# The softmax loop of a two-layer graph network with sixteen slots for gathered rows and indices made eleven groups ahead

## The chip, the cores and the metric

The kernel runs on one core of a Trainium2 chip. The metric is the device time of one execution, in microseconds; lower is better. Three runs are given for the kernel before.

## The reference

There are 6250 nodes with 128 features and 100,000 edges, sorted by destination. Two layers follow each other, each added to its input and normalised:

```python
def L0(h, e, fc_w, attn, rel, src, dst):
    f = (e @ fc_w.T).reshape(-1, 4, 128)
    feat = jnp.sum(jax.nn.leaky_relu(attn[rel] * f, negative_slope=0.2), axis=1)
    return jax.ops.segment_sum(h[src] + feat, dst, num_segments=h.shape[0])

def L1(features, edge_index, W, b, a1_w, a1_b, a2_w, a2_b):
    h = features @ W.T + b
    s1, s2 = h @ a1_w + a1_b[0], h @ a2_w + a2_b[0]
    src, dst = edge_index
    e = s1[src] + s2[dst]
    e = jnp.where(e >= 0, e, 0.01 * e)
    m = jax.ops.segment_max(e, src, num_segments=n)
    ex = jnp.exp(e - m[src])
    att = ex / jax.ops.segment_sum(ex, src, num_segments=n)[src]
    return jax.ops.segment_sum(att[:, None] * h[dst], src, num_segments=n)

x = layernorm(x + L0(x, edge_attr, fc_w, attn, edge_type, src, dst))
x = layernorm(x + L1(x, (src, dst), W, b, a1_w, a1_b, a2_w, a2_b))
```

## The kernel before

Five engines run a program each and meet at semaphores. In the profile PE is TensorE, DVE is VectorE, ACT is ScalarE, POOL is GpSimd and SP issues plain transfers. The kernel has three parts: the edge loop (the first layer, and the sorting of the edges by source), a middle that normalises and computes the rows `h` with the two scores of each node, and the softmax loop (the second layer), followed by the last normalisation.

The softmax loop goes over groups of 512 edges (`TG` = 4 tiles of 128) that belong to one block of 122 source nodes. All groups take the same path:

- ScalarE copies the four index columns of a group into `idx1` (`idx`, L668), `AHEAD` = 5 groups before the group's own step, and counts that in `i1_ready`. It also copies the block's score (`block_s1`, L674).
- GpSimd (`group1`, L546) waits for `i1_ready` and for `o_done` of the group eight before, whose slot it takes, and issues four indirect transfers. Each gathers 128 rows of `h_rows`, 130 floats wide, into slot `k` of `hg`, and adds to `g_in[k]` as it lands.
- TensorE (`rows`, L885) waits for the landing and spreads the destination scores over a 128 by 512 tile, two groups ahead of the group's own step. VectorE takes the maximum over it (`maximum`, L1306), with a penalty that ScalarE made (L682) from a membership matrix (`members`, L1263).
- VectorE updates the running maximum. TensorE (`back`, L896) sends it back to the edges. Two steps later VectorE forms the exponents (`edge_parts`, L1279, and on), ScalarE takes the exponential and scales the gathered rows in their slot (`scale`, L701).
- Three steps later TensorE sums the scaled rows by source (`attend`, L906) and counts `o_done`. Five steps later VectorE adds that into the block's result (`update`, L1273). `o_done` frees the slot for GpSimd at the same time.

Each engine works through its own steps in a fixed order. In step g TensorE does `rows(g + 2)`, `back(g)`, `attend(g - 3)`; VectorE does `update(g - 5)`, then the maximum of g and the exponents of g - 2, then `members(g + 2)`; ScalarE does `idx(g + 5)`, `penalty(g + 2)`, then `probs` and `scale` of g - 2, then `decays(g - 1)`. The sums and maxima of two successive groups use two PSUM areas in turn (`rows_of`, `back_of`, `sums_of`).

`hg` has `S1` = 8 slots in the tile `room`. The tile `arena` holds `h_sb`, the rows as they were computed, until they are written to `h_rows`; the result of the loop stands behind them. The number of groups is known only at run time: it is the number of live groups, rounded up to a multiple of `S1`, and the code is written out for `G1_LEAST` groups but for one stretch in a loop, whose count is read from `more_groups`.

## Time and profile before

| | us |
|---|---|
| median of three runs | 3019.51 |
| lowest and highest | 3010.88, 3020.82 |
| the profiled execution's own time | 2996.43 |
| its span, first to last instruction | 2994.6 |
| softmax loop, first gather to last update | 1666.67 to 2943.45 |

The profile is of one execution. The chain of work that ended last is cut short in this page, at the last few instructions, so it says nothing here; the timeline has to be read in its place. A start in the timeline is when an engine began an instruction; the idle time in brackets is how long it had nothing to do before, with what ended that by the semaphore records. "remote" and "issue" name no instruction. The ends of TensorE's records are modelled. Waits that GpSimd spends are not named: its idle time is put down to "issue".

### The profile page before, as it was taken

The numbers are of one execution on the slowest core, as the hardware profiler recorded it, in microseconds if no ns is written. First come the engines' busy times: TensorE is split into PE (matmuls) and PEld (weight loads), VectorE is DVE, ScalarE is ACT, GpSimd is POOL, SyncE is SP. The second block draws the span as 40 slices with busy tenths as digits, with TensorE's granted clock in tenths as the row PEclk, the third lists the DMA queues.
The fourth block names the chain that finished last, engine by engine and source line by source line (L and its number), as shares of the span: only waits on it lengthen the run. The fifth ranks groups of instructions, "written<-read, shape, count | busy, mean of one in ns | idle before, by whom it ended". The sixth has DMA issues, their size and how long they took to land. (4 is left out here: it accounts for less than half of the span.)

```text
span 2994.6 us, 44539 instructions
## 1 busy us (share of the span) xinstructions
PE 2386.8 (80%) x11705; PEld 1541.4 (51%) x11705; DVE 2350.5 (78%) x5910; ACT 1525.4 (51%) x4524; POOL 2000.6 (67%) x1839
## 2 busy tenths in 40 slices
PE   5899999999999999999997366666666666666662
PEld 2355555555555555555555355555555555555551
DVE  8899999999999999999999455555554555555557
ACT  0366666666666666666665334343343433443433
POOL 0388788778887888888785566666666666666660
PEclk9999999999999999999999665566655666666665
DMA  2233333333333333333332323332232222333322
GB/s 87 67 98 99 95 97 98 99 99 96 97 97 99 98 97 96 96 99 99 99 95 63 79 67 69 65 69 66 65 68 66 68 66 66 69 67 67 66 61 47
DMA packets 156606, 244.12 MB, mean 82 GB/s; under 512 B 40837, under 2 KB 84399, under 8 KB 156227
## 3 DMA queue, kind: packets, MB, share of 16 engines
q0 software_dynamic: 58624, 108.72, 16.7%
q1 hardware_dynamic: 97730, 132.55, 15.3%
q8 instruction: 97, 1.59, 0.2%
q14 instruction: 155, 1.26, 0.1%
HBM read 231.99 MB, written 9.12 MB: 81 GB/s over the span
## 5 line engine op out<-in xcount | busy, mean ns | idle before, releaser
L503 POOL DMA_INDIRECT room<-in_x,pks x784 | 1013.5, 1293 | 351.8 <-issue 238.3
L546 POOL DMA_INDIRECT room<-h_rows,idx x832 | 785.0, 943 | 476.6 <-issue 457.6
L798 PE MATMUL FP<-fc_sb,room 128*128 128x512 f32 x1568 | 834.5, 613 | 4.5 <-DMA room<-in_e 4.5
L597 ACT ACTIVATE w_sb<-WP 128x512 f32<-128x512 f32 x784 | 468.1, 597 | 502.6 <-PE WP L807 306.0
L885 PE MATMUL FP<-ident,room 128*128 128x128 f32 x1664 | 385.8, 405 | 359.2 <-DMA room<-h_rows,idx 224.8
L807 PE MATMUL WP<-at_p,rel_oh 100*128 100x512 bf16 x2352 | 637.7, 379 | 1.7 <-issue 1.7
L885 PEld LDWEIGHTS FP<-ident,room 128*128 128x128 f32 x1664 | 332.4, 297 | 410.6 <-DMA room<-h_rows,idx 255.2
L682 ACT ACTIVATE accT<-accT,neg_big 128x512 f32<-128x512 bf16 x208 | 150.0, 721 | 762.6 <-DVE accT L1263 417.1
L807 PEld LDWEIGHTS WP<-at_p,rel_oh 100*128 100x128 bf16 x2352 | 228.3, 97 | 546.9 <-issue 452.4
L1111 DVE TENSOR_TENSOR z<-FP,w_sb 128x1024 f32<-128x1024 f32 x392 | 479.9, 1224 | 20.8 <-issue 12.3
L1118 DVE SCALAR_TENSOR_TENSOR y<-z 128x2048 f32<-128x2048 f32 x196 | 447.9, 2285 | 0.0
L798 PEld LDWEIGHTS FP<-fc_sb,room 128*128 128x128 f32 x1568 | 267.6, 190 | 70.5 <-DMA room<-in_e 4.7
L701 ACT ACTIVATE room<-room,pr 128x129 f32<-128x129 f32 x832 | 266.6, 392 | 6.8
L1126 DVE TENSOR_TENSOR hs<-y 128x1024 f32<-128x1024 f32 x196 | 238.4, 1216 | 0.0
L604 ACT ACTIVATE boh<-arena,rank_pay 128x52 f32<-128x52 bf16 x784 | 237.2, 375 | 0.0
L514 POOL DMA_INDIRECT sorted_edges<-runs,ridx x196 | 184.1, 939 | 64.9 <-issue 60.8
L817 PEld LDWEIGHTS AP<-doh,room 128*128 128x128 f32 x1568 | 206.3, 192 | 35.2 <-DVE room L1142 6.8
L1273 DVE SCALAR_TENSOR_TENSOR arena<-arena,decay,FP 128x129 f32 x104 | 36.0, 346 | 214.6 <-remote 131.1
L817 PE MATMUL AP<-doh,room 128*128 128x64 f32 x1568 | 197.4, 269 | 6.6 <-DVE accT L1102 4.4
L1273 DVE SCALAR_TENSOR_TENSOR arena<-arena,decay,AP 128x129 f32 x104 | 35.9, 346 | 204.0 <-remote 142.8
L1306 DVE CUSTOM_DVE_ANT_0 hs<-accT,FP 128x512 f32<-128x512 f32 x208 | 141.8, 682 | 29.4 <-issue 21.8
L1263 DVE TENSOR_TENSOR accT<-z,WP 128x512 bf16<-128x512 bf16 x208 | 141.5, 681 | 0.7 <-DVE room L1256 0.7
(222 smaller groups left out, 3071.2 us busy)
## 6 DMA issues: line engine op xcount, KB each, us to landing
room<-in_e SPq DMA_DIRECT2D x196, 256.0 KB
rel_sb<-in_rel_g SPq DMA_DIRECT2D x196, 200.0 KB
z<-sorted_sources SPq DMA_DIRECT2D x208, 128.0 KB
room<-h_rows,idx POOLq DMA_INDIRECT x832
room<-in_x,pks POOLq DMA_INDIRECT x784
sorted_edges<-runs,ridx POOLq DMA_INDIRECT x196
accT<-in_x_t SPq DMA_DIRECT2D x1, 3125.0 KB, 9.8
h_rows<-arena SPq DMA_DIRECT2D x13, 227.5 KB, 2.8
```

The costliest lines, as they stand in the source:

```text
L503: pool.indirect_dma_start(xg[:, k, u, 0:P], None, x[:, :], bass.IndirectOffsetOnAxis(ap=pks[:, k, u:u + 1], axis=0)).then_inc(xg_in[k], 16)
L546: pool.indirect_dma_start(hg[k][:, u, :], None, h_dram[:, :], bass.IndirectOffsetOnAxis(ap=idx1[:, k, u:u + 1], axis=0)).then_inc(g_in[k], 16)
L597: nc.scalar.activation(w_sb[:, u // 2, u % 2, :], WP[u % 2][:, :], ACT.Copy).then_inc(w_copied, 1)
L604: ins = nc.scalar.activation(boh[:, k % 2, u, :], onehot[:, :, bass.ds(g * TG + u, 1)].rearrange("p b o -> p (b o)"), ACT.Identity, bias=0 ...
L701: nc.scalar.activation(hg[k][:, u, 0:P + 1], hg[k][:, u, 0:P + 1], ACT.Identity, bias=0.0, scale=pr[:, k % 2, u:u + 1]).then_inc(h_scaled, 1)
L798: mm = pe.matmul(FP[u // 2][:, u % 2, :], e_sb[:, k, u, :], fc_sb[:, :], start=True, stop=True)
L807: mm = pe.matmul(WP[u % 2][:, :], rel_oh[:, k % 2, u * P:(u + 1) * P], at_p[:, j, :], start=(j == 0), stop=(j == 2))
L817: mm = pe.matmul(AP_[:, 0:W], msg[:, k % 2, u, :], doh[:, k % 2, u, :], start=(u == 0), stop=(u == TG - 1))
L885: mm = pe.matmul(rows_of(k)[:, u * P:(u + 1) * P], hg[k][:, u, P + 1:P + 2].to_broadcast([P, P]), ident[:, :], start=True, stop=True)
L1111: v.tensor_tensor(z[:, h, :, :], FP[h][:, :, :], w_sb[:, h, :, :], ALU.mult).then_inc(z_done, 1)
L1118: v.scalar_tensor_tensor(y[:, :, :, :], z[:, :, :, :], SLOPE0, z[:, :, :, :], ALU.mult, ALU.max).then_inc(y_done, 1)
L1126: v.tensor_tensor(hs[:, :, :], y_all[:, :, 0:D4 // 2], y_all[:, :, D4 // 2:D4], ALU.add).then_inc(hs_done, 1)
```

## The change

`S1` becomes 16 and `AHEAD` 11. Eight of the slots stay in `room`; the other eight lie in `arena`, over `h_sb`, which is dead once its rows are written and its last column is transposed (`n_s1t`, for which GpSimd now waits before its first gather). Each slot has its own semaphore and its own column set of `idx1` and `mparts`. The written-out stretches and the loops are rearranged for multiples of sixteen; the waits that count through a slot's semaphore use `G_IN` (4 a group) in place of 8. VectorE's loop had four steps a pass and registers for the slot; now it has sixteen steps and fixed slots. `LAG`, the number of PSUM areas and the order of each engine's step stay.

```diff
-G1 = 8 * -(-(G0 + NS) // 8)
-G1_LEAST = 8 * -(-G0 // 8)
+S1 = 16
+G1 = S1 * -(-(G0 + NS) // S1)
+G1_LEAST = S1 * -(-G0 // S1)
...
-S1 = 8
 LAG = 5
-AHEAD = 5
-D1 = 4
+AHEAD = 11
+IN_ROOM = 8
+G_IN = 16 * TG // S1
...
-        hg_all = room[:, 0:S1 * TG * HROW].rearrange("p (s u k) -> p s u k", s=S1, u=TG)
-        hg = [hg_all[:, k, :, :] for k in range(S1)]
+        hg = [f[:, j * TG * HROW:(j + 1) * TG * HROW].rearrange("p (u k) -> p u k", u=TG)
+              for f, n in ((room, IN_ROOM), (arena, S1 - IN_ROOM)) for j in range(n)]
...
             more = group_count(pool)
+            pool.wait_ge(n_s1t, 1)
             for k in range(S1):
                 group1(k, k, True)
-            for g in range(S1, G1_LEAST):
+            for g in range(S1, G1_LEAST - S1):
                 group1(g, g % S1, False)
-            with pool.Fori(G1_LEAST, pool.snap(more + (G1_LEAST - S1 + 1)), S1) as i:
+            with pool.Fori(G1_LEAST - S1, pool.snap(more + (G1_LEAST - S1 + 1)), S1) as i:
...
-                    act.wait_ge(g_in[k], 16 * TG + (g - k - S1) * 8)
+                    act.wait_ge(g_in[k], 16 * TG + (g - k - S1) * G_IN)
...
-                pe.wait_ge(g_in[k], 16 * TG + (g - k) * 8)
+                pe.wait_ge(g_in[k], 16 * TG + (g - k) * G_IN)
...
-            with dve.Fori(G1_LEAST - S1, dve.snap(more + (G1_LEAST - 2 * S1 + D1 + 1)), D1) as i:
-                half = dve.snap(i & (S1 - D1))
-                other = dve.snap(S1 - 2 - half)
-                for k in range(D1):
-                    step1(i + k, k, False, half + k, half + (k - 2) if k >= 2 else other + k)
+            with dve.Fori(G1_LEAST - 2 * S1, dve.snap(more + (G1_LEAST - 2 * S1 + 1)), S1) as i:
+                for k in range(S1):
+                    step1(i + k, k, False, k, (k - 2) % S1)
```

The loops of SP, ScalarE and TensorE are changed in the same way as GpSimd's.

## Rows read from the trace of the kernel before

**Rows 1.** Windows: PE, PEld, DVE, ACT, POOL busy (instructions), PEclk, DMA, GB/s.

```profile
200.00:1500.00 1300.00, 1300.00 (x6138) 674.32 (x6137) 1292.82 (x1534) 858.74 (x2215) 1039.66 (x852) 1.00 0.36 97
1800.00:2800.00 1000.00, 635.78 (x3316) 568.75 (x3315) 542.05 (x2813) 393.59 (x1489) 626.83 (x665) 0.61 0.30 67
```

**Rows 2.** Grouped lines, 1800 to 2800 us; last, all gathers on the page.

```profile
L546 POOL DMA_INDIRECT room<-h_rows,idx x665 | 627.2, 943 | 372.3 <-issue 372.3
L885 PE MATMUL FP<-ident,room 128*128 128x128 f32 x1328 | 307.5, 404 | 267.3 <-DMA room<-h_rows,idx 162.0 <-DVE vmax L1306 79.5 <-issue 25.3
...
L1273 DVE SCALAR_TENSOR_TENSOR arena<-arena,decay,FP 128x129 f32 x83 | 28.7, 346 | 183.0 <-remote 119.7 <-PE AP L906 52.7 <-issue 10.6
...
L1273 DVE SCALAR_TENSOR_TENSOR arena<-arena,decay,AP 128x129 f32 x82 | 28.3, 346 | 166.4 <-remote 120.6 <-PE FP L906 41.5 <-issue 4.2
...
L546 POOL DMA_INDIRECT room<-h_rows,idx x832 | 785.0, 943 | 476.6 <-issue 457.6
```

**Rows 3.** Timeline, 2110 to 2152 us: start, duration, idle before in brackets.

```profile
2110.95 2.07 PE L885 MATMUL FP<-ident,room 128*128 128x128 f32 x8 [4.18 <-DMA room<-h_rows,idx]
...
2112.97 2.07 PE L906 MATMUL FP<-room,hs 128*128 128x129 f32 x8
...
2117.44 0.94 POOL L546 DMA_INDIRECT room<-h_rows,idx  x1 [0.30 <-issue]
...
2120.78 0.35 DVE L1273 SCALAR_TENSOR_TENSOR arena<-arena,decay,FP 128x129 f32 x1 [8.05 <-remote]
...
2121.40 0.94 POOL L546 DMA_INDIRECT room<-h_rows,idx  x1 [3.02 <-issue]
...
2128.32 2.08 PE L885 MATMUL FP<-ident,room 128*128 128x128 f32 x8 [2.31 <-DMA room<-h_rows,idx]
...
2130.34 2.07 PE L906 MATMUL AP<-room,w_sb 128*128 128x129 f32 x8
...
2138.78 0.35 DVE L1273 SCALAR_TENSOR_TENSOR arena<-arena,decay,AP 128x129 f32 x1 [1.83 <-remote]
...
2139.40 0.94 POOL L546 DMA_INDIRECT room<-h_rows,idx  x1 [3.32 <-issue]
...
2151.53 0.94 POOL L546 DMA_INDIRECT room<-h_rows,idx  x1 [2.45 <-issue]
```

**Rows 4.** Timeline of the loop's start: GpSimd, VectorE and TensorE.

```profile
1666.67 1.04 POOL L546 DMA_INDIRECT room<-h_rows,idx  x1 [5.22 <-issue]
...
1685.04 0.29 PE L896 MATMUL EP<-mparts,accT 128*128 128x6 bf16 x4
...
1694.22 0.69 DVE L1306 CUSTOM_DVE_ANT_0 hs<-accT,FP 128x512 f32<-128x512 f32 x1 [11.35 <-issue]
...
1704.57 0.18 DVE L1279 TENSOR_REDUCE sm<-EP 128x8 f32<-128x24 f32 x1 [9.65 <-remote]
...
1705.53 0.94 POOL L546 DMA_INDIRECT room<-h_rows,idx  x1 [0.30 <-issue]
...
1711.83 0.69 DVE L1306 CUSTOM_DVE_ANT_0 hs<-accT,FP 128x512 f32<-128x512 f32 x1 [4.84 <-issue]
...
1714.76 0.68 DVE L1306 CUSTOM_DVE_ANT_0 hs<-accT,FP 128x512 f32<-128x512 f32 x1
...
1717.52 0.94 POOL L546 DMA_INDIRECT room<-h_rows,idx  x1 [11.04 <-PE AP L906]
...
1717.94 0.68 DVE L1306 CUSTOM_DVE_ANT_0 hs<-accT,FP 128x512 f32<-128x512 f32 x1
```

**Rows 5.** Timeline of GpSimd's group 16, its last gather, and the last update.

```profile
1764.89 0.94 POOL L546 DMA_INDIRECT room<-h_rows,idx  x1 [0.30 <-issue]
...
2922.07 0.94 POOL L546 DMA_INDIRECT room<-h_rows,idx  x1 [0.30 <-issue]
...
2943.10 0.35 DVE L1273 SCALAR_TENSOR_TENSOR arena<-arena,decay,FP 128x129 f32 x1 [1.28 <-PE FP L906]
```

**Rows 6.** Timeline of ScalarE: an index copy.

```profile
2140.54 0.19 ACT L668 ACTIVATE idx<-y 128x4 int32<-128x4 int32 x1
```

More of the change, by code:

```diff
@@ L194, in build @@
         mT = accT[:, 0:SLOTS * GE // 2].bitcast(BF16).rearrange("p (s k) -> p s k", s=SLOTS)
-        pen = accT[:, S1 * GE // 2:S1 * GE // 2 + SLOTS * GE].rearrange("p (s k) -> p s k", s=SLOTS)
-        hg_all = room[:, 0:S1 * TG * HROW].rearrange("p (s u k) -> p s u k", s=S1, u=TG)
-        hg = [hg_all[:, k, :, :] for k in range(S1)]
+        pen = accT[:, SLOTS * GE:2 * SLOTS * GE].rearrange("p (s k) -> p s k", s=SLOTS)
+        hg = [f[:, j * TG * HROW:(j + 1) * TG * HROW].rearrange("p (u k) -> p u k", u=TG)
+              for f, n in ((room, IN_ROOM), (arena, S1 - IN_ROOM)) for j in range(n)]
         z_flat = z[:, 0, :, :].rearrange("p a k -> p (a k)")
@@ L218, in build @@
         ge = msg_flat[0:NS, 2 * G1:3 * G1]
-        s1_parts = msg_flat[:, TG * HROW:TG * HROW + 2 * G1].bitcast(BF16)[:, 0:G1 * PARTS3].rearrange(
+        s1_parts = msg_flat[:, TG * HROW:TG * HROW + 3 * G1 // 2].bitcast(BF16)[:, 0:G1 * PARTS3].rearrange(
             "p (g c) -> p g c", c=PARTS3)
@@ L472, in _ @@
             more = group_count(sp)
-            for g in range(RSLOTS, G1_LEAST):
+            for g in range(RSLOTS, G1_LEAST - S1):
                 sources(g, g % S1, False)
-            with sp.Fori(G1_LEAST, sp.snap(more + (G1_LEAST - S1 + 1)), S1) as i:
+            with sp.Fori(G1_LEAST - S1, sp.snap(more + (G1_LEAST - S1 + 1)), S1) as i:
                 for k in range(S1):
@@ L725, in _ @@
                 step1(k, k, True)
-            for g in range(S1, G1_LEAST - S1):
+            for g in range(S1, G1_LEAST - 2 * S1):
                 idx(g + AHEAD, (g + AHEAD) % S1, False)
@@ L729, in _ @@
                 step1(g, g % S1, False)
-            with act.Fori(G1_LEAST - S1, act.snap(more + (G1_LEAST - 2 * S1 + 1)), S1) as i:
+            with act.Fori(G1_LEAST - 2 * S1, act.snap(more + (G1_LEAST - 2 * S1 + 1)), S1) as i:
                 for k in range(S1):
@@ L922, in _ @@
                 step1(k, k, True)
-            for g in range(S1, G1_LEAST - S1):
+            for g in range(S1, G1_LEAST - 2 * S1):
                 step1(g, g % S1, False)
-            with pe.Fori(G1_LEAST - S1, pe.snap(more + (G1_LEAST - 2 * S1 + 1)), S1) as i:
+            with pe.Fori(G1_LEAST - 2 * S1, pe.snap(more + (G1_LEAST - 2 * S1 + 1)), S1) as i:
                 for k in range(S1):
@@ L1285, in edge_sum @@
                 v.tensor_tensor(el[:, 0, :], sm[:, :, 0],
-                                hg_all[:, bass.ds(at, 1), :, P + 1].rearrange("p o u -> p (o u)"),
+                                hg[at][:, :, P + 1],
                                 ALU.add).then_inc(edge_summed, 1)
@@ L1382, in _ @@
                 step1(k, k, True, k, k - 2)
-            for g in range(S1, G1_LEAST - S1):
+            for g in range(S1, G1_LEAST - 2 * S1):
                 step1(g, g % S1, False, g % S1, (g - 2) % S1)
-            with dve.Fori(G1_LEAST - S1, dve.snap(more + (G1_LEAST - 2 * S1 + D1 + 1)), D1) as i:
-                half = dve.snap(i & (S1 - D1))
-                other = dve.snap(S1 - 2 - half)
-                for k in range(D1):
-                    step1(i + k, k, False, half + k, half + (k - 2) if k >= 2 else other + k)
+            with dve.Fori(G1_LEAST - 2 * S1, dve.snap(more + (G1_LEAST - 2 * S1 + 1)), S1) as i:
+                for k in range(S1):
+                    step1(i + k, k, False, k, (k - 2) % S1)
             for k in range(S1):
```

## The prediction

> **What bounds the kernel now.** I read the windows of the two large loops first, then the grouped lines of the softmax loop with the waits ahead of them, and at last its timeline. The edge loop is full of arithmetic: VectorE works 1292.82 of 1300 us and TensorE all of it. In the softmax loop no engine is full: in 1000 us VectorE works 542 us, TensorE 636, GpSimd 627, and the granted clock is 0.61, that is, mostly the lower of its two levels, 1.2 GHz [rows 1]. In those 1000 us 665 gathers are issued, four to a group, so a group takes 6.0 us. A gather is 943 ns on GpSimd and stands 0.30 us behind the one before it when nothing holds it, 1.25 us in all, 5.0 us a group. The idle time ahead of the gathers is 372.3 us; 665 x 0.30 = 200 of it is that spacing and 172 are pauses, 1.0 us a group [rows 2].
>
> The same rows name two suspects. TensorE waits 162.0 us for gathered rows to land before L885 (0.97 us a group), and VectorE is idle 183.0 + 166.4 = 349 us before the update L1273, which needs the sum of TensorE (o_done) [rows 2]. The timeline tells what kind of wait the second is. By its count L1273 at 2120.78 is group 67's; TensorE's sum for that group, L906, began at 2112.97 and ends by its record at 2115.04. VectorE goes on 5.7 us after that, and GpSimd starts group 75 at 2121.40, 0.6 us after VectorE: both had waited for the same count. GpSimd's last gather had ended at 2118.38. The same is seen at 2138.78 and 2139.40, for the L906 that ended at 2132.41 [rows 3]. So a slot is not late because TensorE works on it; TensorE's completion becomes visible late, some 2.3 us after GpSimd has stopped issuing gathers. I call this the late signal. What causes it inside the chip no row tells. The rows of GpSimd in 1780 to 2300 us, counted in the timeline, come as bursts of 4, 8 or 12 gathers; a burst of 12 with its pause takes 18.0 us (2121.40 to 2139.40), one of 8 takes 12.1 us (2139.40 to 2151.53): 1.50 and 1.52 us a gather. A longer burst has a longer pause behind it [rows 3].
>
> The start of the loop is the run that matters most here. There eight slots are empty and GpSimd issues 32 gathers without a pause, 1666.67 to 1706.47. In these 40 us VectorE takes the maxima of three groups only, by its count: it stands 11.35 us before the third, at 1694.22, and 9.65 us before L1279 at 1704.57, whose sums TensorE had ended by its record at 1685.33. Once GpSimd is silent the maxima follow each other in 1714.76 to 1717.94, 3.2 us. GpSimd itself then waits 11.04 us for the first slot [rows 4]. Rows gathered far ahead did not make the arithmetic faster; the arithmetic stood still while they were gathered.
>
> **The change, part by part.** (1) *Slots, steady state.* GpSimd may run 16 groups ahead of the sums in place of 8. Since it is paced at 5.0 us and the loop at 6.0, it runs to its limit wherever that lies, and then it waits for the newest sum, as now. What goes is TensorE's wait for landings: two of the six L885 groups from 2110 to 2140 show it, with 4.18 and 2.31 us [rows 3]. The gain has bounds: at most 0.97 us a group (all of the 162 us), at least nothing. VectorE's waits in the same stretch, 8.05 and 1.83 us, end with the late signals [rows 3], and the pace was 1.5 us a gather for each length of burst. So I take the lower bound, no gain. Where the stall goes: TensorE's early maxima row is late no more, and the next thing late is again the sum's signal.
>
> (2) *The first burst.* It grows from 32 gathers to 64: 39.80 us becomes 64 x 1.25 = 80 us, so it ends at 1746.6. Indices do not stop it: eleven exist at once, and the next five need about the steps that VectorE managed in the burst before. Then GpSimd waits for the first sum. A pause of 11.04 us stood behind 32 gathers, 3.32 behind 12 [rows 3, 4]; for 64 I take 11 again (3 if the arithmetic got far enough in 80 us, 20 if the delay doubles with the burst). Group 16 then starts at 1757.6; now it starts at 1764.89 [rows 5]. GpSimd gains 7.3 us.
>
> (3) *The end.* After GpSimd's last gather, which ends at 2923.01 now, the arithmetic behind it takes until 2943.45, that is 20.4 us [rows 5]. With eight more groups standing gathered it has eight more steps to do, at 3.18 us of the undisturbed pace in [rows 4]: 25.4 us more. Bounds: 3.18 a step and, if TensorE at the low clock is the pace (L885 2.07, L896 0.29, L906 2.07 [rows 3, 4]), 4.4, which is 35 us.
>
> (4) *Small edits.* ScalarE makes six more index copies and constant copies before the loop; at 0.19 us each [rows 6] they stand in its wait for VectorE before 1666, and if that cover is gone they cost 2 us once. The wait of GpSimd for the transposition falls before its wait for the table's last writes: nothing. The number of groups is 208 in both (832 gathers divided by four is a multiple of sixteen [rows 2]), so no padding group is added. VectorE's loop over slots, one pass of sixteen in place of passes of four, has the same instructions: nothing, or a few tenths.
>
> Sum: 192 groups at the present pace 0, the start -7.3, the end +25.4, so +18 us. The profiled execution took 2996.43 us around a span of 2994.6; with the change it would be 3014.5. The runs shown lie 23 us above it, median 3019.51, so I forecast 3019.5 + 18 = 3037.5 us, 0.6% slower. A difference under 0.3%, 9 us, is about what a measurement of this kernel can't tell from no change (the three runs lie 10 us apart).
>
> The Trainium skill speaks for the change: "DMA: Bandwidth & Descriptors", section "Rules for kernel authors", says to issue a DMA early, do the work, and wait for it late, so that its fixed cost is overlapped. The landings in [rows 2] agree with it; the first burst in [rows 4] doesn't show the work being done meanwhile. By that rule alone the case would be rival A below.
>
> **Rivals.** A, *the landing wait was the pace*. Of groups three apart each waits for its gather, and each such gather waited for the sum that stood behind the maxima before it: a ring of slot, gather, landing, maxima, sum, 18 us long, that eleven groups of distance would open. For it: groups 72 and 75 (L885 at 2110.95 and 2128.32) waited for landings, three groups apart, and the pace is 18.0 us for three groups whatever the bursts [rows 3]. Against it: the late signal is most of that ring. If all of the 0.97 us goes, the pace is 5.0 us, which is GpSimd's too: 192 x 0.97 = 186 us less, +18, so 2851 us. If a third goes, 62 less, so 2975 us. It decides from 0.1 us a group upward.
>
> B, *fewer pauses*. In a burst of 32 with only as long a pause as a signal needs (5.4 us to L1306 at 1711.83), a group would take 45.4/8 = 5.7 us, so 192 x 0.3 = 58 us less: 2980 us. Against it: during that burst the arithmetic did three groups, not eight [rows 4].
>
> C, *the index becomes the wait*, on the slow side of my forecast. Indices were made three steps before a slot came free; with eleven against sixteen that is one step. ScalarE makes the index copy behind the penalty and scaling of the step before: the copy at 2140.54 comes 1.8 us after the update at 2138.78 whose sum frees the slot at the same distance [rows 3, 6]. Of the two restarts of GpSimd in the cycle the one at 2139.40 would start 1.8 us later; the copy for the one at 2121.40 was made before it. That is 1.8 us in five groups, 0.36 a group, 69 us: 3107 us. It decides where the copy ends after the signal and GpSimd has nothing queued. Against it: the pause lets the arithmetic go on, so half may come back (3070 us).
>
> D, *the burst starves the arithmetic for longer*: the pause behind 64 gathers is 20 us and the pace of the first 50.85 us (6.36 a group) returns now and then. One fifth of the time at it is 192 x 0.33 x 0.2 = 13, and 9 more in the pause: 3060 us.
>
> E, *the change doesn't take hold*: index counts keep GpSimd at its old distance. Then neither start nor end moves and the time is 3019. The eleven ready indices speak against it.
>
> **How the numbers follow.** Forecast (no steady gain, longer end) 0.42, its own range 3015 to 3055; A in full 0.08, A in part or B 0.25; C 0.12; D 0.08; E 0.05. Inside the forecast a tenth of a microsecond of gain per group eats the 18 us, so of its 0.42 I give 0.04 to faster, 0.13 to the same and 0.25 to slower. Faster: 0.04 + 0.33 = 0.37. Same: 0.13 + 0.05 + 0.01 of D = 0.19. Slower: 0.25 + 0.12 + 0.07 = 0.44. For 8 times in 10 the range goes from 2930 (A at half) to 3085 (C between its two values).
>
> **What would show it.** Right: an unbroken row of about 64 gathers at the start with fewer than eight maxima in it; then bursts with pauses as before, 133 gathers in 200 us; TensorE's wait for landings gone; L1273 still waiting for about 350 us in 1000; 40 to 50 us from the last gather to the last L1273. Wrong: over 140 gathers in 200 us and shorter waits at L1273 (A, B); GpSimd starting right behind L668 (C). If the late signal goes away when GpSimd no longer waits for it, my whole argument from the first burst falls.

## The result and the profile after

The changed kernel takes 3086.43 us (median of four runs, 3075.85 to 3092.7), the kernel before beside it 3017.56 (four runs, 3010.88 to 3020.82). The ratio is 1.023, with a 95% interval of 1.0208 to 1.0252: the change makes the kernel slower by 69 us. The forecast was 3037 us with a range to 3085, so the sign was right, the size was not, and the time lies a little over the range. The profile of the changed kernel is that of the execution of 3092.0 us.

The first view is that of the windows, with the columns of [rows 1].

```profile
200.00:1500.00 1300.00, 1298.45 (x6123) 671.74 (x6121) 1285.23 (x1531) 854.10 (x2208) 1039.73 (x850) 1.00 0.35 97
1800.00:2800.00 1000.00, 509.85 (x3171) 469.27 (x3172) 522.16 (x2689) 377.51 (x1425) 595.24 (x632) 0.67 0.28 64
```

The edge loop is as before. In the 1000 us of the softmax loop 632 gathers are issued in place of 665 [rows 1]: 6.33 us a group in place of 6.0. The granted clock isn't the reason: it is 0.67 in this stretch, and was 0.61. The grouped lines of the same stretch, which answer to [rows 2]:

```profile
L547 POOL DMA_INDIRECT arena<-h_rows,idx x320 | 301.9, 943 | 201.0 <-issue 98.7 <-ACT idx L670 51.1 <-remote 26.6
L547 POOL DMA_INDIRECT room<-h_rows,idx x312 | 294.3, 943 | 203.9 <-issue 98.3 <-ACT idx L670 71.6 <-remote 33.6
L887 PE MATMUL FP<-ident,room 128*128 128x128 f32 x640 | 125.7, 360 | 98.6 <-DVE vmax L1308 80.1 <-issue 18.5
L887 PE MATMUL FP<-ident,arena 128*128 128x128 f32 x624 | 119.8, 353 | 90.3 <-DVE vmax L1308 70.1 <-issue 20.0
...
L1275 DVE SCALAR_TENSOR_TENSOR arena<-arena,decay,FP 128x129 f32 x79 | 27.2, 344 | 154.1 <-remote 122.7 <-PE AP L908 27.0 <-issue 4.4
L1275 DVE SCALAR_TENSOR_TENSOR arena<-arena,decay,AP 128x129 f32 x79 | 27.2, 344 | 125.0 <-remote 107.6 <-PE FP L908 17.4
```

Two things are to be seen. TensorE's wait for landings (162.0 us of [rows 2]) is gone altogether; before L887 it waits for VectorE's maxima only. And the idle time ahead of the gathers, 372.3 us before, is 404.9 now, and its releasers name ScalarE's index copy L670 for 122.7 us of it; before they named "issue" alone. Such a wait is put down by the records of the counts, and in this trace many of these are missing (below, at e8). So I also looked at the starts themselves.

A restart is here a group whose first gather stands more than 0.45 us behind the gather before it. From 1800 to 2800 us the kernel before has 73 of them, and each starts 0.3 to 0.6 us behind the end of a VectorE update, the one of the group whose slot it takes: update and gather had waited for the same count, and its own index copy had ended at least 9.6 us earlier. The changed kernel has 79, and 50 of them start 0.81 to 0.85 us behind the end of their own index copy.

The timeline of the loop's start (GpSimd, VectorE's maxima, ScalarE's index copies), which answers to [rows 4]:

```profile
1687.51 0.69 DVE L1308 CUSTOM_DVE_ANT_0 hs<-accT,FP 128x512 f32<-128x512 f32 x1 [2.52 <-issue]
...
1702.22 0.69 DVE L1308 CUSTOM_DVE_ANT_0 hs<-accT,FP 128x512 f32<-128x512 f32 x1 [12.29 <-issue]
...
1735.22 0.69 DVE L1308 CUSTOM_DVE_ANT_0 hs<-accT,FP 128x512 f32<-128x512 f32 x1 [20.24 <-issue]
...
1747.61 0.94 POOL L547 DMA_INDIRECT arena<-h_rows,idx  x1 [0.30 <-issue]
...
1750.17 0.19 ACT L670 ACTIVATE idx<-y 128x4 int32<-128x4 int32 x1
...
1751.14 0.94 POOL L547 DMA_INDIRECT arena<-h_rows,idx  x1 [2.58 <-issue]
...
1764.10 0.69 DVE L1308 CUSTOM_DVE_ANT_0 hs<-accT,FP 128x512 f32<-128x512 f32 x1 [15.43 <-issue]
...
1768.61 0.19 ACT L670 ACTIVATE idx<-y 128x4 int32<-128x4 int32 x1
...
1769.61 0.94 POOL L547 DMA_INDIRECT room<-h_rows,idx  x1 [13.78 <-PE FP L908]
```

GpSimd issues the 60 gathers of groups 0 to 14 without a break, from 1673.80 to 1748.55. In that stretch VectorE takes four maxima, at 1682.55 and at the first three of these rows, 33 us apart at the worst. Group 15 starts at 1751.14, 0.78 us after its index copy has ended (1750.36); group 16 at 1769.61, 0.81 us after its own. So for the sixteenth and the seventeenth group it is the index that GpSimd waits for.

The timeline of the steady state, 2146 to 2189 us, which answers to [rows 3]:

```profile
2146.99 0.35 DVE L1275 SCALAR_TENSOR_TENSOR arena<-arena,decay,AP 128x129 f32 x1 [1.85 <-remote]
...
2148.78 0.19 ACT L670 ACTIVATE idx<-y 128x4 int32<-128x4 int32 x1
...
2149.78 0.94 POOL L547 DMA_INDIRECT arena<-h_rows,idx  x1 [5.41 <-ACT idx L670]
...
2163.46 0.19 ACT L670 ACTIVATE idx<-y 128x4 int32<-128x4 int32 x1
...
2163.52 0.94 POOL L547 DMA_INDIRECT arena<-h_rows,idx  x1 [0.30 <-issue]
...
2167.25 0.35 DVE L1275 SCALAR_TENSOR_TENSOR arena<-arena,decay,FP 128x129 f32 x1 [6.71 <-remote]
...
2167.87 0.94 POOL L547 DMA_INDIRECT arena<-h_rows,idx  x1 [3.40 <-remote]
...
2185.39 0.35 DVE L1275 SCALAR_TENSOR_TENSOR arena<-arena,decay,AP 128x129 f32 x1 [1.82 <-remote]
...
2187.17 0.19 ACT L670 ACTIVATE idx<-y 128x4 int32<-128x4 int32 x1
...
2188.17 0.94 POOL L547 DMA_INDIRECT room<-h_rows,idx  x1 [5.40 <-ACT idx L670]
```

By its count the burst from 2149.78 is that of groups 76 to 78, 12 gathers. It starts 0.81 us after the copy at 2148.78 has ended. The next one, group 79, at 2167.87, had its copy at 2163.46 already: it starts 0.62 us after VectorE's update at 2167.25, that is with the late signal of TensorE's sum, just as all restarts did before [rows 3]. The one at 2188.17 is again 0.81 us behind a copy, at 2187.17. From one index restart to the next are 38.4 us for six groups. Each of the two copies stands 1.8 us behind an update (2146.99, 2185.39), the distance that rival C took from the trace of before; GpSimd starts 2.8 us behind that update and not 0.6.

The end, which answers to [rows 5], GpSimd's last gather and VectorE's last update:

```profile
2984.40 0.94 POOL L547 DMA_INDIRECT arena<-h_rows,idx  x1 [0.30 <-issue]
...
3033.62 0.35 DVE L1275 SCALAR_TENSOR_TENSOR arena<-arena,decay,FP 128x129 f32 x1 [1.37 <-PE FP L908]
```

From the end of the one to the end of the other are 48.6 us; they were 20.4.

The two spans differ by 95.6 us. Of it 7.1 lie ahead of the loop, -2.4 from the first gather to group 16 (95.8 in place of 98.2 us), 57.6 in the 192 groups behind it (0.30 us each), 28.2 in the end, and 5.1 behind the loop. The 7.1 aren't the change's: in e9, the same kernel, the loop starts at 1668.13. The medians differ by 69: the profiled execution of before was 21 us faster than its median, that of after 6 us slower. A second pair (below, e9 and e11) has no such offset and gives the same picture.

The 5.1 us behind the loop are the change's own. From the last update to the last output transfer's issue both kernels take the same 44 us. What grows is GpSimd's closing drain, the last thing but semaphores in the program (duration in ns, before and after):

```profile
L63 POOLq DRAIN  x1: 3912/3912/3912, 2990.5 to 2990.5; - x1
L64 POOLq DRAIN  x1: 9138/9138/9138, 3080.8 to 3080.8; - x1
```

It is 3.91 us in each of the seven traces with eight slots and 9.14 us in each of the thirteen with sixteen, on all chips. What in the kernel makes it longer no run tells; the sixteen-slot kernels also have eight semaphores more.

### The profile page after: what moved, and what is told of

Read it like the earlier page. It is cut to its first block and busy times, and to the rows that moved or that the text cites. A ratio compares the mean times of both kernels' runs of the same rounds, so it can differ in the third digit from the quotient of the medians.

```text
span 3090.2 us, 44656 instructions
## 1 busy us (share of the span) xinstructions
PE 2268.6 (73%) x11705; PEld 1443.1 (47%) x11705; DVE 2349.7 (76%) x5910; ACT 1522.8 (49%) x4524; POOL 2002.6 (65%) x1839
## 5 line engine op out<-in xcount | busy, mean ns | idle before, releaser
L547 POOL DMA_INDIRECT room<-h_rows,idx x416 | 392.5, 944 | 276.9 <-issue 133.8
L547 POOL DMA_INDIRECT arena<-h_rows,idx x416 | 392.4, 943 | 255.3 <-issue 132.4
L887 PE MATMUL FP<-ident,room 128*128 128x128 f32 x832 | 167.2, 366 | 171.2 <-DVE vmax L1308 108.5
L887 PE MATMUL FP<-ident,arena 128*128 128x128 f32 x832 | 155.6, 347 | 114.3 <-DVE vmax L1308 89.4
L887 PEld LDWEIGHTS FP<-ident,room 128*128 128x128 f32 x832 | 150.1, 270 | 186.9 <-issue 157.2
L515 POOL DMA_INDIRECT sorted_edges<-runs,ridx x196 | 191.0, 975 | 64.9 <-issue 60.2
L819 PEld LDWEIGHTS AP<-doh,room 128*128 128x128 f32 x1568 | 205.4, 192 | 37.9 <-DVE room L1144 10.0
L887 PEld LDWEIGHTS FP<-ident,arena 128*128 128x128 f32 x832 | 138.6, 252 | 130.3 <-issue 117.2
```

The source lines that it names most:

```text
L515: pool.indirect_dma_start(table[:, :], bass.IndirectOffsetOnAxis(ap=ridx[:, k:k + 1], axis=0), runs[:, k, :], None).then_inc(sc_in[k], 16)
L547: pool.indirect_dma_start(hg[k][:, u, :], None, h_dram[:, :], bass.IndirectOffsetOnAxis(ap=idx1[:, k, u:u + 1], axis=0)).then_inc(g_in[k], 16)
L819: mm = pe.matmul(AP_[:, 0:W], msg[:, k % 2, u, :], doh[:, k % 2, u, :], start=(u == 0), stop=(u == TG - 1))
L887: mm = pe.matmul(rows_of(k)[:, u * P:(u + 1) * P], hg[k][:, u, P + 1:P + 2].to_broadcast([P, P]), ident[:, :], start=True, stop=True)
```

## The experiments

The kernels ran on five chips, two or four on each, and each ratio is to runs of the kernel before on the same chip. On three of these chips the kernel before takes 2997 to 3008 us. On the two others it takes 2778.5 and 2779.2, and what I called the late signal isn't there; this is told in its place. Pace is the time from group 16 to the last gather, divided by 192; end is the time from the last gather to the last update.

**e1: indices thirteen ahead** (the changed kernel with one number changed).

```diff
-AHEAD = 11
+AHEAD = 13
```

> The changed kernel with indices made thirteen groups ahead in place of eleven, so that the index is again three groups ahead of the slot, as before the change. If the index copy is what gathers wait for in the steady stretch (GpSimd's restart names L670 and the pace is 6.33 us a group), the pace goes back to 6.0 us and 192 x 0.3 = 58 us come back: about 3025 to 3030 us, still 8 to 15 us over the kernel before for the longer end. If instead it is the longer unbroken burst or the place of the slots that makes the loop slow, the pace stays 6.3 us and the time 3080 us or more.

3015.86 us, ratio 1.0062 (1.0046 to 1.0079). Grouped lines, 1800 to 2800 us:

```profile
L547 POOL DMA_INDIRECT arena<-h_rows,idx x342 | 322.6, 943 | 194.2 <-issue 194.2
L547 POOL DMA_INDIRECT room<-h_rows,idx x324 | 305.6, 943 | 180.5 <-issue 180.5
...
L1275 DVE SCALAR_TENSOR_TENSOR arena<-arena,decay,FP 128x129 f32 x84 | 29.0, 346 | 198.2 <-remote 179.2 <-PE AP L908 16.4 <-issue 2.6
...
L1275 DVE SCALAR_TENSOR_TENSOR arena<-arena,decay,AP 128x129 f32 x83 | 28.7, 345 | 167.2 <-remote 142.8 <-PE FP L908 20.1 <-issue 4.2
```

The index copy is gone from the releasers, 666 gathers are issued, as before, and there is still no wait for landings. Pace 6.01 us, end 42.9 us. Two more indices take away all that the steady state had lost; what remains is 18.6 us, near the 18 that the forecast made up of the first burst and the end. All 78 restarts stand behind an update again, and none behind its copy.

**e15: indices twelve ahead.**

```diff
-AHEAD = 11
+AHEAD = 12
```

> The changed kernel with indices twelve groups ahead, one more than the change has. The copy then stands behind the scaling fifteen groups back, in the step in which the sum of the group sixteen back is made. Theory 1, one step more is enough for the slot to be the wait again: 6.0 us a group, ratio 1.004 to 1.008. Theory 2, the copy is still the last thing in most restarts, by 1 to 2 us: 6.15 to 6.3 us a group, ratio 1.012 to 1.022.

3014.62 us, ratio 1.0063 (1.0047 to 1.008); 667 gathers in 1000 us, pace 6.01, end 42.9. One more index is enough.

**e3, e12, e14, e13: indices five, nine, seven and three ahead** (the changed kernel; the line stands for all four).

```diff
-AHEAD = 11
+AHEAD = 5
```

> The changed kernel with sixteen slots and indices only five groups ahead: the slot can never be the wait, the index always is, and no more than about five groups stand gathered. If a release by the index is slow by itself, the pace is 6.3 us or slower (3075 us and more) though the first burst and the end are short (end about 20 us). If the long burst and what it leaves are the cause, the pace is 6.0 us and the time that of the kernel before.

> The changed kernel with indices nine groups ahead in place of eleven, for the second time. With late signals: theory 1, each group of distance lost costs 0.14 us a group: 6.6 us a group, ratio 1.035 to 1.042. Theory 2, the distance from the scaling that releases the index (AHEAD + 3 = 12) counts by its rest against GpSimd's cycle of three groups: 6.0 us a group, ratio 1.002 to 1.006. Without late signals: 1.002, and nothing is told apart.

> The changed kernel with indices seven groups ahead, between two slow ones (5: 7.17 and 9: 7.09 us a group). Theory 1 (distance from index to slot): 7.1 us a group, ratio 1.065 to 1.075. Theory 2 (distance 10 from the scaling, no multiple of four, like 6 and 14 which gave 6.06 and 6.29): 6.0 to 6.3 us a group, an end between 26 and 30 us, ratio 1.000 to 1.022.

> The changed kernel with indices three groups ahead. Theory 1, what counts is how far the index's copy lies behind the first sum that leaves the slot free (S1 - AHEAD): then 3 of 16 is the worst of all, over 7.15 us a group, ratio over 1.07. Theory 2, what counts is the distance from the scaling that releases the index to the gather (AHEAD + 3) against the length in which GpSimd's rows of gathers fall: 3 ahead was 6.06 us a group with eight slots and is the same with sixteen, bursts of twelve, ratio 0.999 to 1.004, while 5 and 9 (distances 8 and 12, multiples of four, bursts of sixteen) stay the slow ones.

The last column is the median time by which a group's index copy starts behind the update that tells of its free slot, from 1800 to 2800 us; below zero, the copy comes first.

| indices ahead | ratio | interval | pace, us | end, us | copy behind slot, us |
|---|---|---|---|---|---|
| 3 | 1.0634 | 1.0571 to 1.0697 | 7.04 | 25.1 | 58.8 |
| 5 | 1.072 | 1.0703 to 1.0738 | 7.11 | 23.7 | 37.9 |
| 7 | 1.0753 | 1.0735 to 1.0771 | 7.05 | 38.2 | 30.2 |
| 9 | 1.0675 | 1.0646 to 1.0705 | 7.03 | 38.3 | 11.5 |
| 11, the change (e9) | 1.0221 | 1.0204 to 1.0238 | 6.29 | 43.8 | 1.6 |
| 12 | 1.0063 | 1.0047 to 1.008 | 6.01 | 42.9 | -6.2 |
| 13 | 1.0062 | 1.0046 to 1.0079 | 6.01 | 42.9 | -12.9 |

The idea that each index lost costs the same is wrong (6.6 us was expected at nine, 7.0 came), and so is the idea of a remainder against GpSimd's cycle, with which I tried twice to explain e2 (below). Three ahead isn't the worst either, as e13's first theory had it. It is a step, and it lies where the copy falls behind the slot's signal. Counted by the code, ScalarE copies an index in its step g, behind `scale(g - 3)` of the step before; the slot for the same group comes free with the sum of group g - 3 in the kernel before and in e1, g - 4 with twelve ahead, g - 5 in the change, g - 7 with nine and g - 11 with five. Up to one step the late signal of the sum still comes after the copy; at two it is the copy that is last in most of the restarts. Of those with a pause of more than 1 us 25 in the change and 28 in e9 stand behind the copy, and they start 44 and 46 us later in all than they would behind the update: 0.28 and 0.29 us a group, about what the pace has lost (0.30 and 0.23). Beyond two steps every restart stands behind its copy (65 of 65 with nine ahead, 39 of 39 with five), and the pace falls to 7.0 to 7.1 and stays there. Grouped lines with five ahead (e3):

```profile
L547 POOL DMA_INDIRECT arena<-h_rows,idx x288 | 271.7, 943 | 243.3 <-PE AP L908 151.6 <-issue 82.7 <-ACT idx L670 9.0
L547 POOL DMA_INDIRECT room<-h_rows,idx x271 | 255.7, 943 | 229.8 <-PE AP L908 125.0 <-issue 77.9 <-ACT idx L670 26.8
...
L1275 DVE SCALAR_TENSOR_TENSOR arena<-arena,decay,AP 128x129 f32 x70 | 24.1, 344 | 465.4 <-remote 465.4
...
L1275 DVE SCALAR_TENSOR_TENSOR arena<-arena,decay,FP 128x129 f32 x70 | 23.8, 340 | 0.6 <-remote 0.6
```

The releaser "PE AP L908" in these lines is not to be believed: all 39 restarts stand 0.81 us behind their index copy, and the slot of each had been free for 40 us and more. GpSimd works here in bursts of sixteen gathers with 8.9 us between them (35 of each in the 1000 us): 15 x 1.25 + 0.94 + 8.9 = 28.6 us for four groups. The idle time before the update is all with one of the two PSUM areas. Why it falls into just this pattern no run settles.

**e10: GpSimd held at fourteen, index at eleven.** The changed kernel with one number more; the slots stay sixteen.

```diff
-                if not lead:
-                    pool.wait_ge(o_done, g - S1 + 1)
+                if k >= REACH or not lead:
+                    pool.wait_ge(o_done, g - REACH + 1)
```

**e11: the same with `REACH` = 8**, and **e9: the changed kernel itself** on the same chip.

> The changed kernel itself beside the kernel before, since the chip of the last four kernels ran the kernel before in 2778.5 us with an unbroken row of gathers (5.0 us a group) and no late signals. If this chip has the late signals (before near 3000): ratio 1.02 to 1.025 and 6.3 us a group. If it hasn't (before near 2780): GpSimd's own 1.25 us a gather is the pace whatever the distance, and what is left is the later start of the loop: ratio 1.002 to 1.003.

> The changed kernel with GpSimd held at fourteen groups ahead of the sums, for the second time, since on the last chip nothing waited for a slot or an index. With late signals (before near 3000): theory 1, the index as the release costs the 0.30 us a group: 6.0 us a group and ratio 1.004 to 1.008, as with indices thirteen ahead (1.006). Theory 2, the long row of gathers costs it: 6.3 us a group and ratio 1.015 to 1.023. Without late signals: 1.002, and nothing is told apart.

> The changed kernel with GpSimd held at eight groups ahead of the sums, for the second time. With late signals: theory 1, distance alone makes the longer end and the small edits and slots cost only the later start: 6.0 us a group, 20 us from the last gather to the last update, ratio 1.002 to 1.004. Theory 2, gathers into two buffers make steps slower: over 6.1 us a group, ratio over 1.008. Without late signals: 1.002 as on the last chip.

| on one chip | ratio | interval | span | group 16 at | pace, us | end, us |
|---|---|---|---|---|---|---|
| e11, held at 8 | 1.0007 | 0.9998 to 1.0017 | 3009.0 | 1768.2 | 6.06 | 20.1 |
| e10, held at 14 | 1.0043 | 1.0026 to 1.0059 | 3020.5 | 1760.0 | 6.08 | 37.2 |
| e9, the change (16) | 1.0221 | 1.0204 to 1.0238 | 3072.0 | 1763.7 | 6.29 | 43.8 |

Grouped lines of e10, 1800 to 2800 us:

```profile
L548 POOL DMA_INDIRECT arena<-h_rows,idx x332 | 313.2, 943 | 192.7 <-issue 192.7
L548 POOL DMA_INDIRECT room<-h_rows,idx x326 | 307.4, 943 | 185.3 <-issue 185.0 <-PE FP L909 0.3
L888 PE MATMUL FP<-ident,room 128*128 128x128 f32 x672 | 143.2, 383 | 131.2 <-DVE vmax L1309 102.8 <-issue 28.0
L888 PE MATMUL FP<-ident,arena 128*128 128x128 f32 x640 | 139.8, 390 | 166.4 <-DVE vmax L1309 120.4 <-issue 45.9
```

In e10 the indices are made eleven ahead as in the change, and nothing is lost in the steady state, for GpSimd now waits for a sum whose signal comes 13 us behind the index copy (median; all 83 restarts start within 0.7 us of the end of that update). So not the number of indices but the index as the last thing to come costs the time. e9 against e11 closes the account: -4.5 us to group 16, +44 in 192 groups, +23.7 at the end: 63, and the spans differ by 63.0. e11 shows that the second buffer and the code for sixteen slots cost nothing in the loop; it has the long drain behind it, as e9 has, so this pair doesn't show that cost. Its median is 2.5 us above the kernel before, which this run can't tell from nothing. It has its landing waits again (86.8 + 78.1 us before L888 in 1000 us), and e10 and e1 have none, at the same pace of 6.0 to 6.1: these waits were not what set the pace.

**e2: indices three ahead in the kernel before** (eight slots).

```diff
-AHEAD = 5
+AHEAD = 3
```

> The kernel before with eight slots and indices made three groups ahead in place of five, so that the index is one group ahead of the slot, the same distance as with sixteen and eleven. If the wait for the index is the cause, this alone gives the slow pace, 6.3 us a group, with the short end: 3017 + 208 x 0.3 = about 3075 to 3085 us. If sixteen slots or the long burst are the cause, it stays within 10 us of the kernel before.

3001.75 us, ratio 1.0017 (1.0007 to 1.0027), pace 6.05 us. I expected 3075 to 3085. Grouped lines:

```profile
L546 POOL DMA_INDIRECT room<-h_rows,idx x661 | 623.5, 943 | 377.3 <-issue 239.5 <-ACT idx L668 44.7 <-PE FP L906 39.1
```

The index copy is named here too, for 44.7 us. In terms of steps, index and slot stand as in the change (step g against the sum of g - 5, in both), and so they do in time: the copy starts 1.6 us behind the update (median). GpSimd's bursts are of twelve gathers in both for the most part (41 in 1000 us here, 42 in e9), but the pause behind them is 3.36 us here and 4.27 in e9 (3.28 behind 27 such bursts before). Restarts behind the copy after more than 1 us are 20 here, and they come 12 us late in all, against 28 and 46 us in e9. That is where the difference lies; why the same five steps delay GpSimd so much less with eight slots isn't settled. By the medians two steps cost 4.5 us here, 0.02 us a group, and 0.23 to 0.30 with sixteen slots.

**e4: plain rows of 512 bytes.** The kernel before with gathers of 128 floats in place of 130. The two score columns are left out of the gathered rows, and ones stand in their place, so the output isn't the reference's.

```diff
-        h_dram = nc.dram_tensor("h_rows", (NX, HROW), F32).ap()
+        h_dram = nc.dram_tensor("h_rows", (NX, P), F32).ap()
...
-                    pool.indirect_dma_start(hg[k][:, u, :], None, h_dram[:, :], bass.IndirectOffsetOnAxis(
+                    pool.indirect_dma_start(hg[k][:, u, 0:P], None, h_dram[:, :], bass.IndirectOffsetOnAxis(
```

> The kernel before, gathering rows of 128 floats (512 bytes) in place of 130 (520 bytes); the two score columns are left out, ones stand in their place, so the output is not the reference's. It asks what makes TensorE's signal late in the softmax loop while none was late in the edge loop, which gathers 512-byte rows. If the split of each row into 512 and 8 bytes is it, the waits before L1273 shrink from 350 us in 1000 to under 100 and the pace drops to 5.0 us a group: about 2810 to 2850 us. If it is the rate at which gathers are issued, whatever their size, the pace stays near 6.0 us and the time within 30 us of the kernel before.

2995.57 us, ratio 0.9995 (0.9985 to 1.0004), pace 6.02, 943 ns a gather. The 8 bytes of a row beyond 512 have no part in the late signals.

**e5, e6, e8: the first runs of e10's, e12's and e11's kernels**, on a chip where the kernel before takes 2778.52 us.

> The changed kernel with one more rule for GpSimd: it may stand at most fourteen groups ahead of the sums (from the fifteenth group on it waits for the sum of the group fourteen back), while the sixteen slots and the indices eleven ahead stay. Now a group's slot comes free behind its index again, though the distance from index to the end of the buffer is as in the changed kernel. Theory 1, the index as the thing that releases GpSimd costs 0.30 us a group: pace back to 6.0 us a group (166 groups in 1000 us), no idle time ahead of gathers put down to the index copy, and an end about 6 x 3.2 = 19 us longer than before: ratio 1.004 to 1.008 (3010 to 3020 beside 2997). Theory 2, the long row of gathers or the slots in the other buffer make each step slower: the pace stays near 6.3 us and the ratio is 1.015 to 1.023.

> The changed kernel with indices nine groups ahead in place of eleven. Both the changed kernel (11: 6.33 us a group) and the one with 5 (7.15) are released by the index. Theory 1, each group of distance lost costs about the same, (7.15 - 6.33) / 6 = 0.14 us: 6.6 us a group, 192 x 0.27 = 52 us more than the changed kernel and an end 6 us shorter: ratio 1.035 to 1.042. Theory 2, a matter of step: the index copy follows the scaling of the group AHEAD + 3 back, and GpSimd works in cycles of three groups; where AHEAD + 3 is a multiple of three (6 with eight slots cost nothing; 12 here) the restarts fall together and the pace is 6.0: ratio 1.002 to 1.006, whereas 14 and 8 are no multiples and were slow.

> The changed kernel with GpSimd held at most eight groups ahead of the sums, as in the kernel before; sixteen slots in two buffers, indices eleven ahead and all small edits stay. Theory 1, the small edits and the place of the slots cost nothing and distance alone makes the longer end: pace 6.0 us a group, 20 us from the last gather to the last update, ratio 0.998 to 1.003. Theory 2, the small edits cost: the loop starts 7 us later as in the changed kernel and the time stays 7 to 12 us above before, ratio 1.002 to 1.004, with the pace at 6.0. Theory 3, gathers into the second buffer are slower: pace above 6.1, ratio over 1.006.

Ratios 1.002 (1.001 to 1.0029), 1.0022 (1.0012 to 1.0032) and 1.0021 (1.0011 to 1.003). Nothing is told apart: all three have a pace of 4.99 to 5.00 us and ends of 19.3 to 20.1. What they have in common is the drain of 9.14 us in place of 3.91; these 5.2 us are most of the 5.4 to 6.5 by which their medians lie above the kernel before. Grouped lines of e8, 1800 to 2300 us:

```profile
L548 POOL DMA_INDIRECT arena<-h_rows,idx x209 | 197.2, 943 | 63.7 <-issue 61.3 <-ACT idx L671 1.2 <-PE FP L909 0.9
L548 POOL DMA_INDIRECT room<-h_rows,idx x192 | 181.2, 944 | 58.5 <-issue 54.5 <-ACT idx L671 2.4 <-PE FP L909 1.2
...
L1276 DVE SCALAR_TENSOR_TENSOR arena<-arena,decay,AP 128x129 f32 x50 | 17.4, 348 | 93.2 <-PE AP L909 93.0
L1276 DVE SCALAR_TENSOR_TENSOR arena<-arena,decay,FP 128x129 f32 x50 | 17.3, 347 | 75.8 <-PE FP L909 75.4
```

GpSimd issues without a break (its idle time, 122.2 us for 401 gathers, is the spacing of 0.30), at the same 944 ns a gather; VectorE's wait before the update ends with TensorE's own L909 and not with "remote". In the first 32 gathers VectorE takes a maximum every 5 us. The trace records when a count is raised, but where signals are late many records are missing. In e8 every count of TensorE and VectorE in the loop is raised within 0.02 us of the end of its instruction (one record of each kind, at the loop's end, has no instruction to it); in the kernel before, from 1800 to 2900 us, 126 of 173 records of `o_done` come more than 0.3 us late, median of all 2.39 us, largest 8.74; in e9 103 of 146, median 2.97, largest 13.2. ScalarE's counts are on time in all of these, as far as they are recorded: of the 183 index copies of that stretch before only 28 have a record. GpSimd's starts 0.81 us behind the copy in the changed kernel bear it out for the copies.

**e16: a breath for GpSimd.** The kernel before with a short memset behind every four gathers; its own count must be there before the next group.

```diff
             def group1(g, k, lead):
+                if not (lead and k == 0):
+                    pool.wait_ge(spaced, g)
                 pool.wait_ge(i1_ready, g + 1)
...
+                pool.memset(iota_i[:, :], 0).then_inc(spaced, 1)
```

e7 is the same kernel on the chip of e8.

> The kernel before, with one memset of 128x256 int32 (some 0.3 us) on GpSimd behind the four gathers of every group. The late signals go with GpSimd issuing gathers without a pause. Theory 1, a short breath of GpSimd after every fourth gather is enough for the signals to be delivered: in the first burst VectorE takes seven or more maxima in place of three, the idle time ahead of the update falls from 349 to under 250 us in 1000, and the pace goes from 6.0 to 5.5 to 5.7 us a group: ratio 0.96 to 0.985. Theory 2, signals are late whenever GpSimd isn't idle for some us: the memset only fills a part of the pauses, the pace stays at 6.0 and the ratio at 0.998 to 1.003. Theory 3: the added time lengthens each burst, 0.3 to 0.4 us a group, 60 to 75 us: ratio 1.02 to 1.025.

> The kernel before with the memset on GpSimd behind every four gathers, for the second time. On the chip without late signals it cost 0.82 + 0.33 - 0.30 = 0.85 us a group (5.92 in place of 5.0 us, ratio 1.069), since the next group waits for the memset's own count. On a chip with late signals: theory 1, that breath of 1.15 us is enough for the signals to be delivered: no longer pauses are left, 5.9 us a group, ratio 0.985 to 0.995. Theory 2, signals stay late as long as gathers are issued, and the memset's own count comes late too: above 6.1 us a group, ratio over 1.01. If before is near 2780 here, 1.069 again and nothing is told.

e7: 2970.02 us, ratio 1.0687 (1.0669 to 1.0705), pace 5.92. e16, on a chip where the kernel before takes 2996.75: 2982.29 us, ratio 0.9953 (0.9937 to 0.997), pace 5.97. The timeline of GpSimd in e16:

```profile
2113.75 0.95 POOL L549 DMA_INDIRECT room<-h_rows,idx  x1 [0.30 <-issue]
...
2114.70 0.33 POOL L551 MEMSET iota_i<- 128x256 int32 x1
...
2115.84 0.95 POOL L549 DMA_INDIRECT room<-h_rows,idx  x1 [0.81 <-issue]
...
2119.60 0.95 POOL L549 DMA_INDIRECT room<-h_rows,idx  x1 [0.30 <-issue]
...
2120.54 0.34 POOL L551 MEMSET iota_i<- 128x256 int32 x1
...
2121.69 0.95 POOL L549 DMA_INDIRECT room<-h_rows,idx  x1 [0.82 <-issue]
```

GpSimd stands 1.15 us between groups (167 of 192 times; 2.2 at the most), and the kernel is faster than before (and than the change, 1.022), although each group now has 0.85 us more of GpSimd's time. In the records of counts none of VectorE's is late any more (50 of 111 for the worst line of the kernel before, L1342, which makes `mparts`); of TensorE's `o_done` 148 of 170 still are, but by less: median 1.87 us. So a breath brings VectorE's signals in time and shortens TensorE's delay, and issuing without a break is at least a part of what makes signals late. In the same chip's terms it is a gain of 0.5%; on a chip without late signals it loses 6.9%.

**e17, e18: a shorter breath, and one for eight gathers.** e17 is e16 with this line; in e18 it stands behind the groups in odd slots only, and counts 2.

```diff
-                pool.memset(iota_i[:, :], 0).then_inc(spaced, 1)
+                pool.memset(iota_ci[:, :], 0).then_inc(spaced, 1)
```

> The kernel before with a memset of 128x1 (0.12 us) in place of 128x256 (0.33 us) behind every fourth gather. If the pause itself and not its length delivers the signals, the pace is GpSimd's own, 5.87 - 0.21 = 5.66 us a group, 192 x 0.35 = 67 us less than before: ratio 0.975 to 0.982 on a chip with late signals. If 0.93 us is too short a breath, signals are late again in part: longer pauses, 5.9 to 6.2 us a group, ratio 0.99 to 1.01. On a chip without late signals (before near 2780): 5.66 in place of 5.0, ratio 1.045.

> The kernel before with that memset of 128x1 behind every eighth gather only. If one breath in eight gathers is enough: (5.66 + 5.0) / 2 = 5.33 us a group, 192 x 0.69 = 132 us less: ratio 0.955 to 0.96 on a chip with late signals. If signals pile up within the ten microseconds of eight gathers, VectorE and TensorE fall behind and GpSimd waits for the sum as before: 5.7 to 6.0 us a group, ratio 0.985 to 1.0. On a chip without late signals: 5.33 in place of 5.0, ratio 1.022.

Both fell on a chip where the kernel before takes 2779.22 us: ratios 1.0515 (1.0498 to 1.0533) and 1.0272 (1.0255 to 1.0289), paces 5.69 and 5.37 us. The price of a breath there is a little above what was expected (1.045 and 1.022), and nothing is said of the late signals. Whether 5.37 us can be had on the other chips, which would beat both kernels, stays open.

## Why the prediction was off, by its own steps

**Step (1), the steady state, failed.** It said that GpSimd would wait for the newest sum, as now, and took no gain and no loss: 192 x 0. Measured: +0.30 us a group in the first pair and +0.23 between e9 and e11, 58 and 44 us. The half about the landings held: the 162 us vanish and nothing is gained, at the lower bound that was taken (e1, e15 and e10 show it without the index). What failed was the tacit part, that a slot stays the last thing to come. That was rival C, given 0.12, and its working was right: one of two restarts comes behind the copy, about 2 us late, 0.36 us a group forecast and 0.23 to 0.30 measured. 3107 us was its full value and 3070 its half; 3086 lies between them, so a sixth to a third of its cost came back, not half. Its count of steps was wrong, though, and made it look weaker than it is: it put the index three steps ahead of the slot before and one ahead now. By the code the copy is made in the step of the very sum that frees the slot before, and two steps behind it now. The copy came 13 us ahead of the signal before and comes 1.6 us behind it now (medians). With that count, and [rows 6] where the copy stands 1.8 us behind the update, C should have been the likeliest case, and not one of eight.

**Step (2), the first burst**: of 60 gathers, not 64, for "indices do not stop it" was wrong for group 15: the maxima had not come far enough. The gain forecast was 7.3 us; it was 2.4 from the first gather on in the first pair and 4.1 in the second (4.5 by the spans). Where the index doesn't stop it, the burst is of 64 and the pause behind it 10.96 us (e1), against 11 taken; group 16 starts 6.4 us earlier than in [rows 5].

**Step (3), the end**: +25.4 forecast, +28.2 measured, +22.5 in e1 and e15, +23.7 between e9 and e11. Right within 3 us. e10, with six more groups in place of eight, has +17.1.

**Step (4), the small edits**: nothing in the loop, right (e11), but the drain behind the kernel wasn't thought of: +5.2 us in every kernel with sixteen slots.

**The sum without step (1)**: +18 us. The kernels with twelve and thirteen indices measure +17.9 and +18.6. That they come so near is partly luck: e15's span against that of before is -7.6 to group 16, -4.1 in the 192 groups, +22.5 at the end and +5.0 behind the loop, together +15.8, so an end shorter by 3 us than forecast and a small gain in the pace cover the drain.

**The rivals.** A is dead: e1 and e15 hide the landing wait wholly and gain next to nothing (6.01 us a group against 6.03). VectorE's idle time before the update grew instead, from 349 to 365 us in e1. The Trainium skill ("DMA: Bandwidth & Descriptors", "Rules for kernel authors") says to issue a DMA early and to wait for it late, so that its fixed cost overlaps with work. These traces agree that the wait goes; they don't show that time is saved where another wait takes its place. B didn't show (the burst and pause of its sum are 45.2 us, not 45.4, which changes nothing): the pace with longer bursts allowed is 6.01 against 6.03. D is not needed: the pause behind 60 gathers was 2.58 and then 13.78 us, and e1's behind 64 was as forecast. E: the change did take hold.

**The late signal** stands on the chips that have it, and the test that the prediction set for it was passed: VectorE takes four maxima in the 75 us of 60 gathers in which GpSimd waits for no sum. What causes it stays open. That it belongs to some chips only no row of one trace could show.

**For the other chips** the same change was run only with a limit on GpSimd's distance (e5, e8) and with fewer indices (e6); neither ever held GpSimd up there, and all cost 0.2%, most of it the drain.

## What to carry to other kernels

A ring of buffers has two releases, the free slot and whatever else its filler needs (an index, an address); when the ring grows, the other release must grow with it, and what to keep is the distance in steps between the two (none before; one more did no harm, two cost 1.6% with sixteen slots, and 0.2% with eight). Sizes that differ by one can lie on either side of such a step: 11, 12 and 13 indices cost 2.2%, 0.6% and 0.6%. A deeper ring costs its depth again at the end, once, if the consumer is slower than the filler: about 3 us for each group here. And where a profile names a releaser, compare the starts too: in e3 it names TensorE's sum for more than half of the idle time, and every restart followed the index.

## What the runs showed of the hardware

On three of the five chips of the experiments, and in the first pair, the counts that TensorE and VectorE raise come late while GpSimd issues indirect gathers without a break: TensorE's sums by 2.39 us in the median before and 2.97 in e9, by up to 13.2. None of ScalarE's recorded counts is late in these two traces, but most of its records are missing. On the two other chips the traces (e5 to e8, e17, e18) have no late count, and the kernel before runs some 220 us faster there, at the same 944 ns a gather; the granted clock of the edge loop is 1.00 in all traces. What differs between these chips no trace tells. A breath of 1.15 us on GpSimd behind every four gathers makes VectorE's counts punctual (e16). A GpSimd that waits starts its next gather 0.81 us behind the end of what raised the count, its own memset (e16) or ScalarE's index copy (e3); without a wait gathers stand 0.30 us apart. GpSimd's closing drain takes 3.91 us in the kernels with eight slots and 9.14 in those with sixteen.
